# First loads reordered onto one queue, later loads of x moved behind the p transposes, and identity multiplies on TensorE ahead of the context

## What is computed

```python
x = x + xattn(layernorm(x), ctx)      # energies = (ctx Wq'+bq)(ctx Wk'+bk)', softmax over rows,
                                      # x_m = layernorm(x) @ attention'
x = x + ffn(layernorm(x))             # bf16_round, layernorm with ln_w, ln_b,
                                      # mx_linear(W1,b1), gelu, mx_linear(W2,b2), residual
```

## Time and profile before

| what | value |
|---|---|
| median of the runs | 290.87 us |
| the profiled execution's own time | 291.86 us |
| its span, first to last instruction | 290.0 us |
| busy: VectorE, TensorE matmul, ScalarE, POOL | 252.4, 228.2, 168.8, 81.2 us |
| mean granted TensorE clock | 0.939 |
| DMA transfers: moved, mean rate | 42.92 MB, 148 GB/s |

### The profile page before, as it was taken

The page is one execution under the profiler, slowest core; times in us unless marked ns, Lnnn a source line. Parts: engine busy times, 40 slices in busy tenths (PEclk is TensorE's granted clock), DMA queues, the critical chain, the costliest instruction groups (busy, mean ns, idle before and its releaser), DMA issues.

```text
span 290.0 us, 3187 instructions
## 1 busy us (share of the span) xinstructions
PE 228.2 (79%) x907; PEld 95.2 (33%) x916; DVE 252.4 (87%) x369; ACT 168.8 (58%) x287; POOL 81.2 (28%) x104
## 2 busy tenths in 40 slices
PE   1386739985998259633699789899999989999882
PEld 0232223432343024211244333344444434444330
DVE  2349999999898899999979999699999999999950
ACT  1218416546895456945986699856655656655300
POOL 1092020022004500043150130841323333444453
PEclk9999798998699959875999999999999999999999
DMA  6996993989778941949652044565453376744851
GB/s 172 379 385 226 222 261 63 239 234 197 137 208 210 205 95 36 214 84 175 110 65 46 0 90 93 100 154 126 88 123 84 86 162 135 155 110 95 162 123 72
DMA packets 103077, 42.92 MB, mean 148 GB/s; under 512 B 93844, under 2 KB 96152, under 8 KB 102552
## 3 DMA queue, kind: packets, MB, share of 16 engines
q1 hardware_dynamic: 99024, 32.78, 54.7%
q10 hardware_dynamic: 3560, 9.97, 10.3%
q0 software_dynamic: 480, 0.02, 0.1%
HBM read 15.48 MB, written 4.19 MB: 68 GB/s over the span
## 4 chain that ended last, share of the span: by engine, by line
DVE 39%; PE 26%; ACT 12%; issue 7%; DMA 7%; POOL 4%; SPq 3%; POOLq 0%; DVEq 0%; ACTq 0%
DVE amax L746 10%; PE ps L649 8%; PE ps L694 6%; PE ps L706 4%; DVE vw L932 3%; DVE w_int L789 3%; DMA cx<-in_ctx 3%; DVE hq L937 3%; DVE pf L853 3%; ACT phl L560 3%; DVE wquant L843 2%; SPq L239 2%; PE ps L652 2%; ACT wst L556 2%; PE ps L629 2%
## 5 line engine op out<-in xcount | busy, mean ns | idle before, releaser
L649 PE MATMUL ps<-pT,xT 128*128 128x512 f16 x192 | 50.4, 419 | 13.7 <-DMA pT<-phl 11.3
L694 PE MATMUL ps<-w1T,cxT 128*128 128x512 bf16 x256 | 58.0, 380 | 0.0
L706 PE MATMUL ps<-w2T,xhl 128*128 128x512 bf16 x247 | 56.7, 380 | 1.6 <-issue 1.0
L556 ACT ACTIVATE wst<-ps 128x1024 bf16<-128x1024 f32 x32 | 32.3, 1019 | 26.1 <-PE ps L694 26.1
L746 DVE TENSOR_REDUCE amax<-phl 128x64 f32<-128x2048 bf16 x16 | 36.5, 2281 | 4.3 <-ACT phl L560 4.3
L649 PEld LDWEIGHTS ps<-pT,xT 128*128 128x128 f16 x192 | 20.3, 107 | 48.1 <-issue 32.4
L416 POOL TENSOR_TENSOR wst<-wst,vs 128x512 bf16<-128x512 bf16 x16 | 18.5, 1158 | 60.4 <-DVE wquant L848 30.8
L637 PE MATMUL ps<-qkT 128*128 128x512 f32 x32 | 18.8, 694 | 20.1 <-ACT pf L457 16.0
L706 PEld LDWEIGHTS ps<-w2T,xhl 128*128 128x128 bf16 x256 | 23.7, 98 | 30.8 <-issue 3.6
L694 PEld LDWEIGHTS ps<-w1T,cxT 128*128 128x128 bf16 x256 | 23.7, 98 | 30.1 <-issue 3.6
L560 ACT ACTIVATE phl<-wst 128x2048 bf16<-128x2048 bf16 x16 | 30.6, 1911 | 1.3
(11 more groups left out here) (75 smaller groups left out, 345.8 us busy)
## 6 DMA issues: line engine op xcount, KB each, us to landing
wst<-in_L_ffn_W ACTq DMA_DIRECT2D x8, 1024.0 KB, 7.3
out_x<-wst SPq DMA_DIRECT2D x16, 256.0 KB, 2.9
xs<-in_x SPq DMA_DIRECT2D x3, 1024.0 KB, 13.9
cx<-in_ctx SPq DMA_DIRECT2D x4, 512.0 KB, 6.8
xs<-in_x ACTq DMA_DIRECT2D x1, 1024.0 KB, 9.0
xhl<-pf SPq DMA_TRANSPOSE x17, 4.3
lnw<-in_L_ffn_ln_w ACTq DMA_DIRECT2D x1, 256.0 KB, 16.0
lnb<-in_L_ffn_ln_b ACTq DMA_DIRECT2D x1, 256.0 KB, 15.8
```

Of the source, the lines that this page charges most:

```text
L556: act.activation(ys[:, k, 1024 * g:1024 * g + 1024], ps_y[:, 2 * g:2 * g + 2, :], ACT.Copy)\
L649: pe.matmul(ps_pv[:, t % 2, :], xT[:, t, NT * a + n, :], pT[:, :, NT * c + n, :], start=(s == 0), stop=False)
L694: last = pe.matmul(ps_y[:, c, :], h1T[:, k, t, :], w1T[:, 4 * c:4 * c + 4, t, :], start=False, stop=(t == KT - 1))
L706: last = pe.matmul(ps_z[:, k, :], h2T[:, k, t, :], w2T[:, t, :], start=False, stop=(t == FT - 1))
```

## The change

SP issues W1 unit 0, x of batch 0 and W2 unit 0 behind its first loads, in this order; ScalarE no longer does. Context 1 is loaded ahead of x of batch 1. x of batches 2 and 3 are loaded behind the p transposes of `front(0)` and `front(1)`. ln_w and ln_b are loaded by ScalarE after its first batch. TensorE multiplies the identity by itself five times before it waits for Wq and Wk, and ten times after their transposition, into PSUM bank 7, which nothing else uses then. VectorE does the first steps of W1 unit 0 ahead of `x_stats(0)`, no longer waits for x of batches 2 and 3 there (`x_stats` has its own wait), and waits for ln_w and ln_b one stage later.

```diff
@@ SP @@
             sp.dma_start(bqk[:, 1:2], bk.rearrange("(d o) -> d o", o=1)).then_inc(ld_bqk, 16)
+            sp.dma_start(wst[:, W1, :].rearrange("p (r k) -> p r k", r=4), w1_t[0]).then_inc(ld_w1, 16)
+            sp.dma_start(xs[:, 0:LT, :], x_t[0]).then_inc(ld_x[0], 16)
+            sp.dma_start(wst[:, W2, :], w2_t[0]).then_inc(ld_w2, 16)
...
-            def front(b, ctx=None):
+            def front(b, ctx=None, later=None):
...
+                if later is not None:
+                    load_x(later)
                 if not isinstance(b, int) or b > 0:
                     w2_transpose(b - 1)
                 w1_transpose(b)
...
+            load_ctx(1)
             load_x(1)
-            load_ctx(1)
-            for b in range(2, B):
-                load_x(b)
             load_ctx(2)
-            front(0)
-            front(1, 3)
+            front(0, None, 2)
+            front(1, 3, 3)
@@ ScalarE @@
-            act.dma_start(xs[:, 0:LT, :], x_t[0]).then_inc(ld_x[0], 16)
-
-            act.dma_start(wst[:, W1, :].rearrange("p (r k) -> p r k", r=4), w1_t[0]).then_inc(ld_w1, 16)
-            act.dma_start(wst[:, W2, :], w2_t[0]).then_inc(ld_w2, 16)
-            act.dma_start(lnw[:, :], ...).then_inc(ld_ln, 16)
-            act.dma_start(lnb[:, :], ...).then_inc(ld_ln, 16)
...
             batch(None, 0, 1, None)
+            act.dma_start(lnw[:, :], ...).then_inc(ld_ln, 16)
+            act.dma_start(lnb[:, :], ...).then_inc(ld_ln, 16)
@@ TensorE @@
+            def keep_busy(n):
+
+                for _ in range(n):
+                    pe.matmul(ps[:, 7, 0:P], ident[:, :], ident[:, :], start=True, stop=True)
+
             pe.wait_ge(c_id, 1)
+            keep_busy(5)
             pe.wait_ge(ld_w, 32)
...
             last.then_inc(wT_ps, 1)
+            keep_busy(10)
@@ VectorE @@
-            x_stats(0)
             w_amax(W1, 0)
             w_power(W1, 0)
             w_scale(W1, 0)
             w_inverse(W1, 0)
+            x_stats(0)
             front(0, None, None, 1, None)
             back(0, 0, 0, None)
-            for b in range(2, B):
-                dve.wait_ge(ld_x[b], 16)
-            dve.wait_ge(ld_ln, 32)
             front(1, 1, 0, 2, None)
             back(1, 1, 1, None)
+            dve.wait_ge(ld_ln, 32)
```

More of the change, by code:

```diff
@@ L432, in _ @@
             act.dma_start(b2f[:, 0, :], b2.rearrange("(j b) -> j b", b=P)).then_inc(ld_b2, 16)
-            act.dma_start(xs[:, 0:LT, :], x_t[0]).then_inc(ld_x[0], 16)
-            act.dma_start(wst[:, W1, :].rearrange("p (r k) -> p r k", r=4), w1_t[0]).then_inc(ld_w1, 16)
-            act.dma_start(wst[:, W2, :], w2_t[0]).then_inc(ld_w2, 16)
-            act.dma_start(lnw[:, :], ln_w.rearrange("(o n) -> o n", o=1).broadcast_to([P, H])).then_inc(ld_ln, 16)
-            act.dma_start(lnb[:, :], ln_b.rearrange("(o n) -> o n", o=1).broadcast_to([P, H])).then_inc(ld_ln, 16)
             act.wait_ge(wT_ps, 1)
@@ L545, in _ @@
             batch(None, 0, 1, None)
+            act.dma_start(lnw[:, :], ln_w.rearrange("(o n) -> o n", o=1).broadcast_to([P, H])).then_inc(ld_ln, 16)
+            act.dma_start(lnb[:, :], ln_b.rearrange("(o n) -> o n", o=1).broadcast_to([P, H])).then_inc(ld_ln, 16)
             batch(0, 1, 2, None)
```

## The result

| | before | changed |
|---|---|---|
| median of 10 runs, us | 290.88 | 289.16 |
| lowest to highest | 289.65 to 294.75 | 287.00 to 289.85 |
| profiled execution (span) | 291.86 (290.0) | 287.00 (285.2) |
| ratio, 95% interval | | 0.9933 [0.9905, 0.9961] |

The changed kernel is faster by 1.7 us as the medians have it and by 1.9 (0.7%) as the ratio has it. Forecast was 286.0, a gain of 4.9: the direction is right, 289.16 lies inside 284.2 to 289.8, and the size is off by a factor of two and a half to three. Ratios leave single disturbed runs out (over 1.5% above the fastest run of their kernel).

A forecast was written before the change was run, and what follows sets the result against it. Mostly VectorE (39%), with the start set by waits before its first steady step. Gain 5.4 us at the start less 0.5 for lnw and lnb, 4.9: 291.86 to 287.0 profiled, median 286.0 us, range 284.2 to 289.8.

The forecast's parts named there:

- Step 1, the context alone: At the start: the context, no longer fetched beside x, W1 and W2, lands at 6.3 us instead of 10.39.
- Step 2, the clock: First products: multiplies raise TensorE's clock, eight records take 3.6 us instead of 6.35, row maximum at 16.2 instead of 21.92.
- x leg: Start: x's load, statistics and POOL's factors, leading to the first normalised tile; forecast to end last, at 17.1 us.
- TensorE leg: Start: context, its transposes, ScalarE's copy, query and key products, energies, to the first row maximum; forecast to end at 16.2 us.
- Step 3: Start, x loaded behind W1: factors ready at 17.1 us, so L920, the first normalised tile, moves from 22.53: 5.4 us gained.
- Step 4, term lnw and lnb: Later stages: lnw and lnb, issued after ScalarE's first batch, hold batch 0's p transposes; cost 0.5 us, between 0 and 2.9.
- the forecast's own case: Whole kernel: the forecast's mechanism holds, time between 285.2 and 288.9 us; chance 0.56.
- Swallowed: Rival: a longer later wait, likeliest at the p transposes of batch 1, takes the gain; 290 to 291 us; chance 0.08.
- Slower, by x ahead of the transposes: Rival: x of batches 2 and 3 holds SP's transposes, 2.85 us a place; 291.2 to 294.0 us; chance 0.08.
- Nothing for the context: Rival at the start: order changes nothing, context still at 10.4, only the clock helps; gain 3.7 (287.2 us); chance 0.03.
- W1 and x early: Rival at the start: W1 at 7.5 and x at 10.1 us, gain 5.7 to 6.6, about 284.8 us; chance 0.10.
- Multiplies stay too long: Rival at the start: 0.9 us a multiply (288.4 us), or the clock stays low (290.4); chance 0.15.

The follow-up runs named there:

- again: The changed kernel unaltered, measured and profiled once more: 289.03 us, ratio 0.9938 [0.9904, 0.9971].
- fill_both: Changed kernel plus 12 identity multiplies ahead of the first value stage, 3 and 4 ahead of batch 0's energies of tiles 2 and 3: 287.82 us, 0.9907.
- best_b: Second run of: changed kernel, x and statistics ahead of W1, lnw/lnb on SP behind first W1 transpose, multiplies spread (6 at start, 2, 2, 8): 289.01 us, 0.9856.
- again_b: The changed kernel unaltered, one execution for a third profile: 288.2 us.
- x_early: Changed kernel with x of batches 2 and 3 again loaded ahead of the transposes, as before the change: 289.53 us, ratio 0.9957.
- combo: Changed kernel, x and statistics ahead of W1, lnw/lnb on ScalarE before its first batch, multiplies spread (6 at start, 2, 2, 8): 287.18 us, 0.9878.
- no_multiplies: Changed kernel without its fifteen identity multiplies, keeping the new order of loads: 288.42 us, ratio 0.9895 [0.9845, 0.9945].

## Why the prediction was right and wrong

**Step 1, the context alone: right.** It lands 4.2, 3.7 and 3.7 us after its issue in the three profiles of the changed kernel, against 7.2 to 8.7 in four of the kernel before; the forecast 6.3 compares with 5.9 and 5.4. Taken strictly, as the prediction weighed it, the rule of the Trainium skill, *DMA: Bandwidth & Descriptors* ("Issuing engines are not separate DMA queues"), that issuing from several engines saves only issue time, would have moved nothing, and that is not what happened. What else the section says, that transfers interleave on the same engines whoever issued them, agrees: beside 3 MB of the other queue the context took twice as long. No run separates the single queue from the place in the order.

**Step 2, the clock: right in mechanism, worth nothing that could be measured.** Multiplies at 0.5 us, eight records in 3.67, maximum at 16.22 (16.2 forecast). But the step's own comparison had the x leg later than this one; without the multiplies the maximum comes at 16.61, still ahead of that leg. The prediction never asked what the TensorE leg would be without them, and so didn't say that this part of the change is idle.

**Step 3 failed at both ends of its difference.** "L920 moves from 22.53 to 17.1": the first number is of an execution with a late context. The prediction took its 1.0 us over the median off once, at the end, as if it lay evenly over the whole kernel and stood in both kernels alike; it lay for the most part in the very transfer that the change repairs, so it had to come off the gain. That is 1.1 us (22.53 - 21.44). The second number came out as 17.99, 0.9 late, because W1 lands at 10.3 to 10.6 and not 9.5. The step had W1's bytes move at 217 GB/s, one load after the other. In the changed kernel's profile they don't (stretch, length, then as above, last the GB/s):

```profile
2.00:4.60 2.60, 2.60 (x14) 2.60 (x14) 1.59 (x8) 1.07 (x1) 0.25 (x2) 1.00 0.87 274
4.60:6.40 1.80, 1.80 (x11) 1.80 (x10) 0.51 (x3) 0.60 (x1) 0.00 (x0) 1.00 0.23 59
6.40:10.60 4.20, 2.93 (x22) 2.73 (x22) 0.00 (x0) 1.02 (x1) 0.00 (x0) 1.00 0.99 331
```

For 1.8 us the engines are nearly idle, at 59 GB/s. The small bq and bk are on their way then (they land 3.4 and 4.5 us after their issues at 2.13 and 2.67), and W1 stands behind them. The prediction had half a microsecond for these parts, and only in its late end for x. And from the start to 10.6 us 2.24 MB are moved (0.03 of them before 2.00), while W1 ends 1.83 MB down the queue: x had begun to move beside it. That bq and bk cause the gap is read from the order of the landings and wasn't tried. 5.4 becomes 3.45.

**Step 4, term lnw and lnb: mis-sized.** Priced at 0.5 inside 0 to 2.9. The runs put it at 1.0 to 1.8, and the three profiles show 1.2 us given back on average, by held p transposes and a longer low-clock stretch (1.5 to 2.0 in two, 0 in the third). The "slack of 1.3 us" set a transpose landing at 43.9 against products at 45.17. In again the products were ready at 41.40 (42.70 less the wait of 1.30), 3.8 us earlier, and the transpose only 1.2 us (42.70). The whole stage moved to the front, the held transpose moved less: the first of the four begins 3.3 us earlier (29.93 against 33.20), but from its begin to the end of the fourth it is 10.6 us instead of 8.5. The step also had no term for the clock, without which the hold costs VectorE next to nothing (fill_both, best_b).

**The whole sum.** 3.45 us at the start, less 1.6 more of later waits in a typical execution (2.3 against 0.7, worked out beside the table), is the 1.7 to 1.9 measured. The prediction had 5.4 less 0.5. The profiles show 1.2 us of the changed kernel's later waits in their places; in which places its median execution spends another microsecond no profile shows, since none was taken of an execution above 288.6. That the result lies inside the range is luck in part: the forecast's own case ended at 288.9, and 289.16 lies beyond it, in the room that the range had for a swallowed gain. Its own signs of being wrong did show: L649's first product less than 4 us before 45.17 (L654 at 42.70 and 42.45 in again and again_b), with p transposes of 4577 and 3987 ns ahead of it.

**Rivals.** "Swallowed", at 0.08, was the right mechanism in part, at the p transposes of batch 0 and not of batch 1. "Slower, by x ahead of the transposes" is refuted by x_early. "Nothing for the context" is refuted. "W1 and x early" did not occur: W1 is late. "Multiplies stay too long" (0.9 us each) did not occur either: they take 0.5. That they outlast the context (8.20 against 5.9) was in the forecast's own sum, and falls on a leg with slack.

**Open:** why the context is late in one of four profiles of before; where a typical execution of the changed kernel loses its last microsecond; why ScalarE's W1 block and the first p transpose are issued together in some executions and apart in others; and the losses near 75 to 80 and 165 to 185 us, which come and go with the low-clock stretches in profiles of every variant.

## What to carry to other kernels

A change worth about 1% at the start of a kernel must be costed against several profiles of it: one profile can hold a transfer that is a microsecond late, and that microsecond belongs to the gain, not to the offset. Find which leg ends last *after* each part of the change; a part that shortens another one is worth nothing. Here two small moves (statistics ahead of W1, so that POOL's factors are made under cover, and lnw and lnb ahead of the first batch) brought 2 us beyond the change, where fifteen multiplies brought nothing that could be measured. Put a load that has no early user where no transpose is issued behind it: two small ones in front of the p transposes cost between half a microsecond and two, more where TensorE's clock is low at the same time. And line the executions up at one instruction: start, constant rest and waits then come apart, and it shows whether a profile is a typical one.

## What the runs showed of the hardware

- The same program on the same data has its low-clock stretches at different places: first rise at 7.4, 5.9 and 5.4 us in the changed kernel, at 19.0, 18.2, 16.3 and 18.0 in the kernel before; in the value stage 38.1 to 44.9, 36.7 to 46.9 and 39.5 to 46.3. The Trainium skill, *TensorE: Matmul & The Clock Gate* (Part 1), says that the number of slow matmuls varies from run to run; these traces agree (the rises are the clock changes that each trace stores): the eight product records of before take 6.35, 6.60, 5.71 and 6.53 us.
- A single 512 KB load took 7.3, 7.2 and 7.3 us in three executions and 8.7 in a fourth, with an unchanged program.
- Beside other loads a p transpose occupies SP's queue for 1310 ns in one case and for 4577 in another of the same batch (again), 6142 at most (combo). A W1 transpose issued behind a 1 MB load in the same queue takes 5.75 and 5.31 us (changed, again), and 1.98 without that load (x_early).
- The column of the granted clock reads 1.00 for the changed kernel's first stretch too, while eight transposes of the context take 1.97 us at 6.11 in no_multiplies and 1.04 us at 8.20 in the changed kernel. The stretch before the first rise is read from the durations of the records, not from the column:

```profile
0.00:6.50 6.50, 4.98 (x23) 4.98 (x24) 2.10 (x10) 1.88 (x2) 1.40 (x9) 1.00 0.44 133
L608 PE MATMUL ps<-ident x30: 274/421/582, 1.5 to 8.1; 128*128 128x128 f32 x30
```

  The second row gives the shortest, middle and longest record of the multiplies: 274 ns at the upper level and up to 582 at the lower.
